# All table tiles gathered by GpSimd, a head of 520 tiles, and an epilogue with x in 13 pieces

## The reference, cut to what matters

```
N, F, R, E = 12500, 64, 64, 200000     # nodes, features, relations, edges; dst is sorted
h   = relu(layernorm(x))                                   # N x 64
W   = einsum('rb,bio->rio', comp, basis)                   # a 64x64 matrix for each relation
s   = segment_sum(h[src] * weight, etype * N + dst)        # R x N x 64
agg = einsum('rni,rio->no', s, W)
y   = relu(agg + bias) + relu(h @ res_w.T + res_b)
out = x + (y - mean(y)) * rsqrt(var(y) + 1e-5) * gamma + beta   # mean, var over the nodes
```

## Time and profile before

| what | us |
|---|---|
| median of 3 runs | 1991.76 (1989.40 to 1994.21) |
| the profiled execution | 1994.12 |
| its span, first to last instruction | 1992.1 |
| busy: PE, POOL, ACT, DVE | 1604.7, 1479.3, 927.1, 923.4 |
| gathers of the head, L528, x512 | 494.3 busy |
| gathers of the table, L555, x1022 | 982.8 busy, 320.4 idle before them |
| idle of PE's weight loads on the two PSUM tiles of L1248, released by a gather | 77.5 and 65.6 |
| mean granted clock of TensorE, share of full speed | 0.729 |

### The profile page before, as it was taken

How to read it: one execution, slowest core, us unless ns; L and a number is a source line. 1 busy time by engine, 2 the same in 40 slices (tenths; PEclk the granted TensorE clock), 3 DMA queues, 4 the chain that set the end, 5 groups by cost and what they waited for, 6 DMA issues and landing times. The chain is left out here.

```text
span 1992.1 us, 36246 instructions
## 1 busy us (share of the span) xinstructions
PE 1604.7 (81%) x6504; PEld 820.8 (41%) x6553; DVE 923.4 (46%) x3200; ACT 927.1 (47%) x2171; POOL 1479.3 (74%) x1548
## 2 busy tenths in 40 slices
PE   4599999999989858988878798888888989845444
PEld 4243444433333335655544453443444434322222
DVE  6631111311100057887846683783856848424223
ACT  4587777777777465555524442452424424000002
POOL 6777777777777677777777777777777777777773
PEclk9999999999999655555566557568667585856556
DMA  9599999999999522222221221221221211111114
GB/s 189 205 401 405 405 406 399 405 405 405 406 401 403 182 43 49 49 55 50 55 39 38 49 49 33 44 55 32 46 44 38 49 33 38 29 27 28 28 27 141
DMA packets 121905, 308.05 MB, mean 155 GB/s; under 512 B 51100, under 2 KB 51319, under 8 KB 96358
## 3 DMA queue, kind: packets, MB, share of 16 engines
q1 hardware_dynamic: 59822, 236.64, 30.4%
q0 software_dynamic: 49088, 50.36, 12.5%
q10 hardware_dynamic: 12768, 18.71, 3.4%
HBM read 79.75 MB, written 225.83 MB: 153 GB/s over the span
## 5 line engine op out<-in xcount | busy, mean ns | idle before, releaser
L555 POOL DMA_INDIRECT shared<-z_table,idx_all x1022 | 982.8, 962 | 320.4 <-issue 237.1
L528 POOL DMA_INDIRECT acc<-in_x,idx_all x512 | 494.3, 965 | 162.8 <-issue 155.8
L1132 PE MATMUL zps<-wp,res 128*128 128x512 bf16 x2303 | 524.4, 382 | 41.6 <-ACT zst L578 28.9
L578 ACT ACTIVATE zst<-zps 128x512 f32<-128x512 f32 (+1 forms) x784 | 411.3, 602 | 149.8 <-DMA z_table<-zst 127.0
L1132 PEld LDWEIGHTS zps<-wp,res 128*128 128x128 bf16 x2352 | 219.0, 98 | 341.3 <-ACT zst L578 99.4
L1262 PE MATMUL mps<-res 128*128 128x160 f32 (+4 forms) x684 | 347.1, 611 | 11.8 <-issue 6.3
L700 ACT ACTIVATE res<-res,hw 128x64 f32<-128x64 f32 x512 | 176.3, 344 | 302.2 <-DVE hw L1035 118.5
L1009 DVE TENSOR_SCALAR shared<-iota,rel_all,wgt_all 128x36 f32<-128x36 f32 (+10 forms) x1051 | 312.5, 324 | 1.1 <-issue 0.9
L1248 PE MATMUL aps<-shared 128*64 128x36 f32 (+10 forms) x1030 | 193.3, 314 | 123.7 <-DVE shared L1009 57.7
L1248 PE MATMUL zps<-shared 128*64 128x36 f32 (+10 forms) x1014 | 188.7, 313 | 98.6 <-DVE shared L1009 40.5
L1248 PEld LDWEIGHTS aps<-shared 128*64 128x64 f32 x1030 | 126.6, 191 | 298.2 <-issue 199.2
(11 more groups left out here) (152 smaller groups left out, 881.4 us busy)
## 6 DMA issues: line engine op xcount, KB each, us to landing
z_table<-zst SPq DMA_DIRECT2D x194, 1024.0 KB, 9.6
wp<-z_table SPq DMA_DIRECT2D x2560, 0.2 KB
wp<-z_table ACTq DMA_DIRECT2D x1152, 0.2 KB
head_rows<-acc SPq DMA_DIRECT2D x64, 256.0 KB, 9.9
shared<-z_table,idx_all POOLq DMA_INDIRECT x1022, 2.5
res<-head_rows ACTq DMA_DIRECT2D x62, 256.0 KB
acc<-in_x,idx_all POOLq DMA_INDIRECT x512, 6.2
zst<-in_x SPq DMA_DIRECT2D x1, 3072.0 KB
```

Source lines behind the costliest of these rows:

```text
L528: e.indirect_dma_start(out=ring[:, b % NRING, i, :], out_offset=None, in_=x, in_offset=bass.IndirectOffsetOnAxis(ap=idx_all[:, t:t + 1], a ...
L555: e.indirect_dma_start(out=ys[:, q % NY, :], out_offset=None, in_=table[:, :], in_offset=bass.IndirectOffsetOnAxis(ap=idx_all[:, col:col + ...
L578: e.activation(to, frm, ACT.Copy).then_inc(s_ez, 1)
L1132: last = e.matmul(to, lhsT=stationary(px, pw), rhs=moving(px, pw), start=(a == 0), stop=(a == 2))
```

## The change

- `HEAD` is 520. Its keys no longer fit 128 partitions of 4 tiles: 512 tiles (`MAIN`) are loaded and transposed as before, and 8 more (`EX`) as 8 rows of their own: four more small loads on ScalarE's queue, their own casts and key steps on VectorE (`keys_of`), and one more transpose each on TensorE.
- VectorE takes the column indices of the head first of all, in two steps; GpSimd starts after the first 64 columns.
- `fetch`, `owner` and all that belongs to them go; GpSimd gathers all 1043 table tiles, with the 36 buffers as before.
- SP loads all 65 head blocks again. After the last head chunk it loads x in 13 pieces, one every 8 tiles from tile 887 on.
- Chunk 11 is done inside the stream, after table tile 1036; its `moments` come in VectorE's list at the last tile.
- GpSimd scales chunks 3, 6, 9 and 12 in the epilogue, ScalarE the other nine.
- Three windows and the ends of the head's chunks are a little wider or later; 4 loads of keys on SP's queue go, since the second group of table keys now has 65 rows.

```diff
-HEAD = 512
-HEAD_ENDS = (209, 296, 362, 418, 467, HEAD)
+HEAD, MAIN = 520, 512
+HEAD_ENDS = (212, 301, 368, 425, 475, HEAD)
-WINS = (36, 40, 46, 50, 54, 60, 64, 68, 72, 76, 82)
+WINS = (36, 42, 46, 50, 54, 60, 64, 70, 72, 78, 82)
-DONE, DONE_STEP = ((176, 9), (187, 11)), 5
-REGS = 32
-SP_EVERY, SP_FIRST, NSP = 50, 58, 3
-ACT_BATCH, ACT_REST, ACT_EPI, ACT_TILES, NACT = 14, 64, 10, 9, 3
-ACT_LATE = 30
+DONE, DONE_STEP = ((176, 9), (187, 11), (194, 12)), 5
+POOL_SCALES = (3, 6, 9, 12)
+X_LATE, X_STEP = 40, 8
+    IDX_FROM = (0, 64)
+    moments_at = [min(t + NOH + 1, NZT - 1) for t in epi_after]
...
@@ SyncE
+            def load_x(n):
+                rows, to = in_runs(x, n)
+                e.dma_start(to, rows).then_inc(s_xre, 16)
...
-                for b in range(2):
-                    e.dma_start(hs[:, b, :, :].rearrange("p i f -> p (i f)"), hd[b, :, :]).then_inc(s_hld[b], 16)
+                for b in range(NHB):
+                    if b >= 2:
+                        e.wait_ge(s_hab, HB * (b - 1))
+                    e.dma_start(hs[:, b % 2, :, :].rearrange("p i f -> p (i f)"), hd[b, :, :]).then_inc(s_hld[b % 2], 16)
+                e.wait_ge(s_rel, NHK)
                 table_landed(e)
-                for j, t in enumerate(tiles_of_queue["sp"]):
-                    if j >= NSP:
-                        e.wait_ge(s_agg, tiles_of_queue["sp"][j - NSP] + 1)
-                    for r in range(P):
-                        fetch(e, regs, t, r, sp_rows[:, j % NSP, :], s_sp[j % NSP])
+                for n in range(NEPI):
+                    e.wait_ge(s_agg, HEAD_UNTIL + X_LATE + n * X_STEP)
+                    load_x(n)
...
@@ GpSimd
             for t in range(HEAD):
+                if t in IDX_FROM:
+                    e.wait_ge(s_hidx, IDX_FROM.index(t) + 1)
...
-                for q, t in enumerate(pool_tiles):
-                    if q >= NY:
-                        e.wait_ge(s_agg, pool_tiles[q - NY] + 1)
+                for t, (col, _, _, _) in enumerate(seq):
+                    if t >= NY:
+                        e.wait_ge(s_agg, t - NY + 1)
...
+            e.wait_ge(s_st, 9)
+            for n in POOL_SCALES:
+                y = acc[:, n * EPI:n * EPI + epi_width[n]]
+                e.tensor_scalar(y, y, bmv[:, 6:7], bmv[:, 8:9], ALU.mult, ALU.add).then_inc(s_scp, 1)
...
@@ ScalarE
             e.dma_start(hsrc_i[0:HR, :], head_rows(src)).then_inc(s_hsrc, 16)
+            e.dma_start(xsrc_i[:, :], extra_rows(src)).then_inc(s_hsrc, 16)
...
+            for to, arr in ((xdst_i, dst), (xety_i, etype), (xlo_f, weight)):
+                e.dma_start(to[0:EX, :], extra_rows(arr)).then_inc(s_hin, 16)
...
-                            fetch_rows(ACT_BATCH * (i + 1) // HB - ACT_BATCH * i // HB)
-                        if n + 2 < NHB:
-                            e.wait_ge(s_hab, HB * (n + 1))
-                            e.dma_start(hs[:, n % 2, :, :].rearrange("p i f -> p (i f)"), hd[n + 2, :, :]).then_inc(s_hld[n % 2], 16)
...
             for n, w in enumerate(epi_width):
+                if n not in POOL_SCALES:
...
@@ VectorE
+            e.wait_ge(s_hrow, 1)
+            take_main(idx_all, 0, IDX_FROM[1] // HC).then_inc(s_hidx, 1)
+            take_main(idx_all, IDX_FROM[1] // HC, HR)
+            e.tensor_copy(idx_all[:, MAIN:HEAD], mflat[:, HC * P:HC * P + EX]).then_inc(s_hidx, 1)
...
@@ in the norm loop
-                    if n[0] == 0:
-                        e.wait_ge(s_hrow, 1)
-                        take_head(idx_all).then_inc(s_hidx, 1)
...
-                        if t - NOH - 1 in epi_after:
-                            moments(epi_after.index(t - NOH - 1))
+                        if t in moments_at:
+                            moments(moments_at.index(t))
```

More of the change, by code:

```diff
@@ L137, in rgcn_kernel @@
     assert done == len(head_items)
[L140 to L171, removed]
     table = nc.dram_tensor("z_table", [NCLS * N * CLS, F], F32)
@@ L223, in rgcn_kernel @@
         xdup = shared[:, 2 * BANK + 2 * LNT * F:4 * BANK + 2 * LNT * F].rearrange("p (s t a f) -> p s t a f", s=2, a=2, f=F)
+        xdst_i, xety_i, xlo_i, xhi_i = (acc_i[:, 4 * 2 * GE + NRING * HB * F + k * P:4 * 2 * GE + NRING * HB * F + (k + 1) * P] for k in range(4))
+        xkey_f, xlo_f, xhi_f = (a.bitcast(F32) for a in (xdst_i, xlo_i, xhi_i))
         base_h, span_h = (acc[0:1, k * HEAD:(k + 1) * HEAD] for k in range(2))
@@ L444, in _, with in_runs @@
                 store_head(b)
+            def in_runs(rows, n):
+                n0, n1, run = n * EPI, min((n + 1) * EPI, N), epi_run[n]
+                return rows[n0:n1, :].rearrange("(i j) f -> i (j f)", j=run), xoflat[0:(n1 - n0) // run, n0 // P * F:(n0 // P + run) * F]
+            def load_x(n):
+                rows, to = in_runs(x, n)
+                e.dma_start(to, rows).then_inc(s_xre, 16)
             flag = fast_path_flag(e)
@@ L471, in _ @@
                 head_stored(e)
-                for b in range(2):
-                    e.dma_start(hs[:, b, :, :].rearrange("p i f -> p (i f)"), hd[b, :, :]).then_inc(s_hld[b], 16)
-                table_landed(e)
-                e.wait_ge(s_met, 3)
-                regs = [e.alloc_register(f"sp_row{k}") for k in range(REGS)]
-                for j, t in enumerate(tiles_of_queue["sp"]):
-                    if j >= NSP:
-                        e.wait_ge(s_agg, tiles_of_queue["sp"][j - NSP] + 1)
-                    for r in range(P):
-                        fetch(e, regs, t, r, sp_rows[:, j % NSP, :], s_sp[j % NSP])
[L482 to L493, removed]
+                for b in range(NHB):
[3 more added lines that the diff above has]
+                e.wait_ge(s_rel, NHK)
+                table_landed(e)
+                for n in range(NEPI):
+                    e.wait_ge(s_agg, HEAD_UNTIL + X_LATE + n * X_STEP)
+                    load_x(n)
             for n in range(NEPI):
@@ L669, in _ @@
                     clear(sacc[:, a:a + 2048]).then_inc(s_flush, 1)
[L670 to L680, removed]
                 for kind, n, *_ in sums:
@@ new lines, in keys_of, with by_tile @@
+            def keys_of(rows, tiles, dst_of, ety_of, mod_of, mask_of, key, lo, hi, low, high):
+                def by_tile(a):
+                    return a[0:rows, :].rearrange("p (c n) -> p c n", c=tiles)
+                e.tensor_reduce(low, by_tile(dst_of), AX, ALU.min)
+                link(e.tensor_reduce(high, by_tile(dst_of), AX, ALU.max))
+                link(e.tensor_tensor(high, high, low, ALU.subtract))
+                e.tensor_scalar(mod_of[0:rows, :], ety_of[0:rows, :], HALF - 1, None, ALU.bitwise_and)
+                link(e.tensor_tensor(by_tile(key), by_tile(dst_of), low.unsqueeze(2).broadcast_to([rows, tiles, P]), ALU.subtract))
+                link(e.scalar_tensor_tensor(out=key[0:rows, :], in0=key[0:rows, :], scalar=float(HALF), in1=mod_of[0:rows, :],
+                                            op0=ALU.mult, op1=ALU.add))
+                link(e.tensor_scalar(mask_of[0:rows, :], ety_of[0:rows, :], float(HALF), None, ALU.is_ge))
+                link(e.tensor_tensor(hi[0:rows, :], lo[0:rows, :], mask_of[0:rows, :], ALU.mult))
+                return e.tensor_tensor(lo[0:rows, :], lo[0:rows, :], hi[0:rows, :], ALU.subtract)
@@ L1094, in bank, with head_tiles @@
                 return bank_of(job)
-            def head_tiles(frm):
+            def head_tiles(frm, extra):
                 for i in range(HC):
-                    last = transpose(mflat[:, i * P:i * P + HR], frm[0:HR, i * P:(i + 1) * P], HR)
-                return last
+                    transpose(mflat[:, i * P:i * P + HR], frm[0:HR, i * P:(i + 1) * P], HR)
+                return transpose(mflat[:, HC * P:HC * P + EX], extra[0:EX, :], EX)
             e.wait_ge(s_cst, 1)
             e.wait_ge(s_hcast, 1)
-            head_tiles(hsrc_f).then_inc(s_hrow, 1)
+            head_tiles(hsrc_f, xhi_f).then_inc(s_hrow, 1)
             e.wait_ge(s_cst, 5)
@@ L1164, in meta @@
                         for i in range(HC):
-                            last = transpose(mps[0:1, k, i * P:i * P + HR], hspan[0:HR, k, i:i + 1], HR)
+                            transpose(mps[0:1, k, i * P:i * P + HR], hspan[0:HR, k, i:i + 1], HR)
+                        last = transpose(aps[0:1, 0, k * EX:(k + 1) * EX], xspan[:, k:k + 1], EX)
                     last.then_inc(s_mt, 1)
@@ L1174, in meta @@
                     e.wait_ge(s_met, 1)
-                    head_tiles({"key": hkey_f, "lo": hlo_f, "hi": hhi_f}[what]).then_inc(s_mt, 1)
+                    head_tiles(*{"key": (hkey_f, xkey_f), "lo": (hlo_f, xlo_f), "hi": (hhi_f, xhi_f)}[what]).then_inc(s_mt, 1)
                 else:
@@ L1282, in _ @@
             for n, w in enumerate(epi_width):
-                e.wait_ge(s_sc, n + 1)
+                pools = sum(k <= n for k in POOL_SCALES)
+                if n in POOL_SCALES:
+                    e.wait_ge(s_scp, pools)
+                else:
```

(1 more changed line is left out.)

116 lines of the change are left out of this document (44 added, 72 removed).

## The result

The changed kernel takes 2012.11 us (median of 4 runs, 2009.81 to 2014.66) against 1992.34 us (4 runs, 1989.40 to 1994.21): ratio 1.0101, 95% interval [1.0085, 1.0117]. It is slower by 19.8 us; I had said 2015 and +23.0. Beside the later kernels, on another chip, it took 2011.92 against 1994.34 us, ratio 1.0086 [1.0070, 1.0103].

A forecast was written before the change was run, and what follows sets the result against it. GpSimd's gather list was taken as the bound. First table gather 671.8, gathers 1320.0 and tail 23.2 summed to a 2015.0 us span, 2014.7 on the median's scale, said as 2015 (+23.0); range 2006 to 2023.

The forecast's parts named there:

- first to last table gather: GpSimd's second stage: 21 more gathers at an unchanged pace of 1.2668 us, 1320.0 us against 1293.4, +26.6 us.
- tail: Last table gather to the end: 23.2 us instead of 29.8, from x early, chunk 11 early and GpSimd's scaling.
- rival 1: Second stage: fetches had slowed the gathers; without them 1.245 us each, end at 1992, no change; chance 0.04.
- the excess over 1.245 us: Gather pace above its floor of 0.944 + 0.30 us: 22 us in all, said to go with VectorE's load.
- the fetches slowed the gathers: Second stage, same as rival 1: pace drops to 1.245 us without fetching, no change in time; chance 0.04.
- rival 4: Start: slip hidden by overlooked slack, first table gather stays at 669, time 2012 us; counted inside the forecast's 0.91.
- The junction: Head to table stage: first table gather at 671.8 us, +3.0, from a +2.0 start slip and +1.0 for more bytes.
- x early: Tail: x loaded in pieces a hundred tiles earlier, clear of the last gathers, -3.5 us (0 to -3.6).
- chunk 11 early: Tail: chunk 11 summed inside the stream, 1.9 us instead of 4.80 from first product to final statistics, -2.9 us.
- GpSimd's scaling: Epilogue: GpSimd scales four of 13 chunks, but VectorE's additions set the end; -0.2 us, at most 0.5.
- the rival of the late chunk: Epilogue: GpSimd's first scaling starts slowly, 6 us, shifting all after chunk 3; 2018 us, inside the forecast's 0.91.

The follow-up runs named there:

- both_more: `both` with 12 tiles fetched by ScalarE instead of 9, so 1012 gathers by GpSimd: 2016.05 us, ratio 1.0097 to the kernel before.
- idle_fetch: Changed kernel with the row-by-row fetching put back but its rows used by nobody, GpSimd still gathering every tile: 2014.07 us, ratio 1.0104 to the kernel before.
- both: Changed kernel with the fetching put back and used (SP 19 tiles, ScalarE 9, GpSimd 1015): 1977.96 us, ratio 0.9925 to the kernel before; again 1980.61, 0.9927.
- late_idx: Changed kernel with the head's column indices taken in one step behind VectorE's first norm step, as before: 2014.58 us, ratio 1.0101 to the kernel before.
- late_x: Changed kernel with its 13 loads of x all released only after table tile 1037 of 1043: 2015.87 us, ratio 1.0112 to the kernel before.

## Why the prediction was right, step by step

| step | predicted | one profile each | mean of two each |
|---|---|---|---|
| first to last table gather | +26.6 | +22.5 | 1292.2 to 1316.0, +23.7 |
| first table gather | +3.0 | +2.1 | 669.9 to 671.2, +1.3 |
| tail | -6.6 | -6.2 | 29.9 to 23.65, -6.3 |
| sum | +23.0 | +18.4 | +18.7 |

- **The bound.** GpSimd's list is the time: shown from both sides, by taking the fetching away from the kernel before (+32.7 us, of which +33.7 between first and last gather) and giving it back to the changed one (-34 us), with no wait of GpSimd for TensorE over 0.3 us in either. `both_more` shows what a real wait looks like. The change gave 29 tiles back to GpSimd, of which 8 go into the head.
- **The gathers, mis-sized by 3 us.** The mechanism and the count were right: 21 gathers more are 26.6 us at 1.2668 us as at 1.2656, the mean of two profiles before. What I had wrong is that the pace stays. It is 1.2629 and 1.2630 in the two profiles after, and 1042 gathers at 0.0027 us less are the 2.8 us that are missing. Some 1.5 us of it may be the fetching that went (see `idle_fetch`), the rest chance: the profile I read had the highest pace of all in which GpSimd never waits. No run settles the shares.
- **What the excess over 1.245 us is.** I had put it down to VectorE's load, from the earlier trace rows. The same two stretches after the change, 800 to 900 and 1740 to 1880 us, don't bear that out:

```profile
L510 POOL DMA_INDIRECT shared<-z_table,idx_all x80 | 76.6, 958 | 24.4 <-issue 18.6 <-PE zps L1198 3.7 <-PE aps L1198 2.1
...
L510 POOL DMA_INDIRECT shared<-z_table,idx_all x112 | 107.4, 959 | 34.1 <-issue 32.0 <-PE aps L1198 1.2 <-PE zps L1198 0.9
```

VectorE was busy 75.2 of 100 us in the first and 46.0 of 140 in the second, and a gather takes 958 and 959 ns. So VectorE's busy share alone doesn't set it. The median gather is 944 ns in both kernels and the mean 958 to 962, so the excess lies in few long ones: 76 gathers before and 65 after are over 1000 ns, and they hold 17.2 and 13.8 us of it. What lengthens these no run took apart, so the earlier trace rows settle neither this nor the rule named beside rival 1.
- **The rival "the fetches slowed the gathers"** needed 1.245 us; the lowest of 14 profiles has 1.2621. The measured 2012 us is also the number of rival 4 (the first gather stays at 669), but not its mechanism: the first gather came 2.1 us later in the first pair of profiles and 0.5 in the second.
- **The junction.** The 8 more head gathers went into the early start and the idle 8.87 us, as worked out, but these were nearly used up: the last head gather starts at 669.2 us instead of 659.0 and ends at 670.1 (I had 667.8), and the table tiles are released 0.8 and 1.7 us after it. The head's pace was 1.2747 us where I had taken 1.270 from one execution; the second profile before has 1.2745. In `both` and `late_idx` GpSimd's side ended last, with 0.30 us before the first table gather. GpSimd's start was 7.61 us (7.3 predicted), ScalarE's 12.12 (12.4), the first store 1.9 us later (2.0). The sum of +3.0 was too much against the mean, since the junction of one kernel moves by 2 us between executions (668.85 and 671.04 before); how much of it the slip and the bytes are, two profiles can't say.
- **The tail.** Undone one by one: x early is worth 4.1 us (3.5 predicted), chunk 11 early 3.1 (2.9), GpSimd's scaling 0.1 (0.2), the last within noise. They add to 7.3 where 6.2 were gained in the first pair of profiles. Half a us of the difference is `late_x`: its pieces ran so late that the last gather was used 6.5 us after its start, against 6.1 in the earlier trace rows. Some 0.4 us is TensorE's granted clock at the statistics, 1.00 of full speed (2.4 GHz) there before and 0.50 (1.2 GHz) after. VectorE waits for their two small products (L1281 and L1231) longer, before and after:

```profile
1975.36 0.16 DVE L1063 COPY bmv<-mps 128x3 f32<-128x3 f32 x1 [0.70 <-PE mps L1281]
...
1993.77 0.16 DVE L1023 COPY bmv<-mps 128x3 f32<-128x3 f32 x1 [1.10 <-PE mps L1231]
```

The second profile before has 0.50 and 1.11 us there too, after the same work of TensorE, so this doesn't hang on the change. From ScalarE's first scaling to the end it takes equally long before (1977.14 to 1992.1 us) and after (1995.55 to 2010.5): of GpSimd's -0.2 nothing shows. GpSimd's four chunks took 2.70 us, 0.765 for a full one (0.8 taken), and began 0.07 us after ScalarE's, with no start-up cost to be seen: the rival of the late chunk is out. The Trainium skill (GPSIMD Engine Reference, Instruction dispatch) has some 6 us for the first call of a freshly loaded routine. This trace shows none for this operation; whether it counts as freshly loaded, no run tells. The Trainium skill's figure for a simple loop over 512 elements, 0.77 us (side-by-side cycle accounting), agrees with the 0.765 us of the trace.
- **What the change brings and loses.** Its edits besides the fetching are worth 15 us when kept together with it (`both` against before): the shorter tail, and 7 table gathers fewer because 8 more tiles go through the head and one fewer is fetched. Dropping the fetching costs 34.

## What to carry to other kernels

When one engine works through a list of equal instructions and no gap in it is over the fixed issue time, that list is the time. Price a change by what it adds to that list, and let the other engines' work count as hidden until a wait shows that their slack has ended. Off-loading is worth its full price per item only up to the point where the helper's own queue delays someone: 28 tiles on SP and ScalarE (9 of them ScalarE's) gained 1.2 us each, the next three on ScalarE cost 35 us together. And take a pace that is to be multiplied by a thousand from more than one execution, both for its size and for whether the change moves it: 0.002 us in it were 2 us here.

## What was not expected

- ScalarE's margin: 4 more row fetches for each block of 8 head tiles, 0.40 us of ScalarE's queue each, turned -3.8 us into +35.
- VectorE's load doesn't explain the gathers' excess over 1.245 us once the same stretches are read after the change.
- The time from the first table store to the table's landing varies by some 2 us between executions of one kernel, about as much as the start-up edits moved it.
